# Attention ramp: spare multiplications on TensorE, two projections moved a quad sooner, maxima loaded behind a stack

## The chip, the cores and the metric

The kernel runs on one core of a Trainium2 chip. The metric is the device time of one execution in microseconds (us). The kernel before has a median of 692.57 us over three runs (691.49 to 697.25).

## The reference

One transformer layer on `x` of shape 8 x 512 x 128, in float32: attention with 16 heads of size 8, a residual and a layer norm, then a mixture of experts (one shared and eight routed, two of them per row) with a residual and a layer norm. Only attention is touched by the change:

```python
qkv = x @ w_qkv + b_qkv
qkv = qkv.reshape(B, 16, S, 24)          # 32 rows of x make one head
q, k, v = jnp.split(qkv, 3, axis=-1)     # head dimension 8
attn = jax.nn.softmax(jnp.einsum('bhqd,bhkd->bhqk', q, k) / sqrt(8), axis=-1)
vals = jnp.einsum('bhqk,bhkd->bhqd', attn, v)
x = layernorm(x + vals.transpose(0, 2, 1, 3).reshape(B, S, 128) @ w_out + b_out)
...                                      # mixture of experts, second layer norm
```

## The kernel before

The 4096 rows of `x` are 32 **quads** of 128 rows; one quad holds four heads of 512 positions, and four quads make one batch. Attention is a software pipeline over **stages**: `run_stages` runs stage -4, -3, ... on all engines, and each engine has its instructions of every stage written out in a fixed order. Stage s = 4b + i does, each where the quad exists:

- the projections of quad s + 4: TensorE turns `x` (job `xT`, L506), ScalarE copies it, TensorE multiplies by `wq` and `wk` (job `qkv`, L512, L513) and, for quad s + 1, by `wv` (L517); ScalarE reads the results (L562, L566);
- the split of quad s + 4 into three bf16 parts on GpSimd (L831 to L837), which waits until the parts of the quad before are stored;
- on SyncE's queue: the load of the next 128 rows of `x` (L706), the store of the parts of quad s + 3 (L745), two small loads of the maxima of quad s + 1 into the row stack (L751), then the reads that build the **stack** of quad s + 3, its `qs` (L763, three) and `ks` (L767, five), from the stored parts, and later the expert weights (L725);
- the A scores of quad s + 2 on TensorE (L987, bf16, 72 rows of the array, 512 columns), of which VectorE takes row maxima (L931), eight steps of two matmuls and one reduction; `scoreA` has two banks, so that the A scores of a step wait for the reduction two steps before;
- the maxima of quad s + 1: TensorE turns them (job `mT`, L524, after step 1), VectorE splits and negates them (L599, L601, behind the reduction of step 1), SyncE loads them (L751);
- the B scores of quad s (L1001, 74 rows: 72 and the two of the maxima), which ScalarE exponentiates (L904), and the product with `v` of quad s - 1, called PV here (L1021, float32, 128 rows, four groups of four matmuls, after steps 1, 3, 5 and 7).

So stages -4 to -1 fill the pipe. Stage -2 is the first with A scores (quad 0), stage 0 the first with B scores, stage 1 the first with PV. All jobs of TensorE share one bank, `shared`: a job begins when the one before was read (`job_read`). Their order is the table in `Jobs.at`, which says at which step of which stage each kind stands.

TensorE begins the A scores of a stage once the stack of that quad has landed (L975), and the B scores once the maxima are loaded (L993). SyncE has one queue in order: what stands behind a wait there waits too.

Of the kernel before, what the change touches and what calls it, by code (L numbers as in the profile page):

```python
# [50 lines left out]
class Jobs:  # L51
# [4 lines left out]

    def __init__(self, batches):
        self.quads = 4 * batches  # L60
        self.batches = batches
        self.index = {}
        n = 0
        for s in range(-4, self.quads + 4):
            for at in range(8):
                for kind in self.at(s // 4, s % 4, at):
                    self.index[kind, s] = n
                    n += 1
        self.total = n
        self.period = self.index["mT", 12] - self.index["mT", 8]  # L70

    def at(self, b, i, at):

        inner = not isinstance(b, int)
        s = 4 * b + i if not inner else 8
        kinds = []
        if at == 0 and i == 2 and (inner or 1 <= b <= self.batches):
            kinds.append("proj")
        if at == 5 and i == 3 and (inner or 1 <= b <= self.batches):
            kinds.append("x1T")  # L80
        if at == 1 and (inner or 0 <= s + 1 < self.quads):
            kinds.append("mT")
        if at == 2 and i == 1 and (inner or 2 <= b <= self.batches):
            kinds.append("counts")
        if at == 3 and (inner or 0 <= s - 2 < self.quads):
            kinds.append("valsT")
        if at == 4 and (inner or s + 4 < self.quads):
            kinds.append("xT")
        if at == 7 and i == 3 and (inner or 1 <= b <= self.batches):
            kinds.append("gate")  # L90
        if at == 6 and (inner or s + 4 < self.quads or 0 <= s + 1 < self.quads):
            kinds.append("qkv")
        if at == 7 and i == 1 and (inner or 1 <= b <= self.batches):
            kinds.append("oT")
        return kinds

    def number(self, kind, b, i):

# [6 lines left out]
def layer(nc, x, w_qkv, b_qkv, w_out, b_out, wg, ws1, ws3, ws2, we1, we3, we2, out):  # L105
# [26 lines left out]
    with ctx:  # L132
# [167 lines left out]
        def has(b, i, ahead):  # L300

            return not isinstance(b, int) or 0 <= 4 * b + i + ahead < QUADS

        def finishing(b):

            return not isinstance(b, int) or 1 <= b <= B
# [391 lines left out]
        def attention_sync(sp):  # L698
            sp.dma_start(w_raw[:], w_qkv.rearrange("i (c k d) -> i c k d", k=3, d=HD)).then_inc(qkv_loaded, 16)

            def load_x(b, i):

                if has(b, i, 2):
                    bb, ii = (b, i - 2) if i > 1 else (b - 1, i + 2)
                    need(sp, job_ready, jobs.number("xT", bb, ii) + 1)
                sp.dma_start(xin[:, i % 2, :], x_rows[bass.ds((4 * b + i + 4) * P, P), :]).then_inc(x_loaded[i % 2], 16)  # L706

            load_x(-1, 0)
            load_x(-1, 1)
            bias = b_qkv.rearrange("(c k d) -> c k d", k=3, d=HD)  # L710
            for k in range(2):
                sp.dma_start(bq[:, k:k + 1], bias[:, k, :].rearrange("c d -> d c"), allow_slow_non_contiguous=True) \
                  .then_inc(bias_loaded, 16)
            bias_low = b_qkv.rearrange("(q l k d) -> l k q d", q=NCH, l=4, k=3)
            for low in range(4):
                sp.dma_start(bv[32 * low:32 * low + 32], repeated(bias_low[low, 2], 32)).then_inc(w_loaded, 16)
            sp.dma_start(w_o[:], w_out).then_inc(w_loaded, 16)
            sp.dma_start(b_o[:], b_out.partition_broadcast(P)).then_inc(w_loaded, 16)
            sp.dma_start(w_g[:], wg).then_inc(w_loaded, 16)

            def load_expert_weights(n):

                if n < 2:
                    w, at = (we1, we3)[n], w13[:, 0:E, n, :]
                    sp.dma_start(at, w.rearrange("e d f -> d e f")).then_inc(experts_loaded, 16)  # L725
                elif n < 2 + NFC:
                    c = n - 2
                    sp.dma_start(w2[:, 0:E, c, :], we2[:, c * P:(c + 1) * P, :].rearrange("e f d -> f e d")) \
                      .then_inc(experts_loaded, 16)
                elif n == 2 + NFC:  # L730
                    sp.dma_start(w13[:, E, 0, :], ws1).then_inc(experts_loaded, 16)
                    sp.dma_start(w13[:, E, 1, :], ws3).then_inc(experts_loaded, 16)
                    sp.dma_start(w2[:, E], ws2.rearrange("(c f) d -> f c d", f=P)).then_inc(experts_loaded, 16)

            def stage(b, i):
                q = 4 * b + i
                if has(b, i, 4) and not (isinstance(b, int) and q < -2):
                    load_x(b, i)
                if has(b, i, 3):

                    n, par = q + 3, (i + 3) % 2
                    need(sp, split_done, n + 1)

                    need(sp, stack_loaded[par], 16 * STACK_DMAS * (2 * b + (i + 3) // 2))
                    sp.dma_start(parts_dram[par].rearrange("k h i p t -> p (k h i) t"),  # L745
                                 parts[:].rearrange("p k h i t -> p (k h i) t")).then_inc(parts_stored, 16)
                if has(b, i, 1):

                    sp.wait_ge(job_read, jobs.number("mT", b, i) + 1)
                    for m in range(2):  # L750
                        sp.dma_start(qs[KR + m:KR + m + 1, (i + 1) % 4].rearrange("p h x -> p (h x)"), m2[:, m, :]) \  # L751
                          .then_inc(m_loaded, 16)
                if has(b, i, 3):
                    need(sp, parts_stored, 16 * (n + 1))

                    if has(b, i, -1):
                        need(sp, b_ready, 16 * q)
                    st = (i + 3) % 4
                    if isinstance(b, int) and n < 4:

                        sp.wait_ge(ones_set, n + 1)
                    for r in range(3):
                        sp.dma_start(qs[PR * r:PR * (r + 1), st],  # L763
                                     parts_dram[par, 0].rearrange("h i (d c) t -> (i d) h (c t)", d=HD)) \
                          .then_inc(stack_loaded[par], 16)
                    for row, i0, i1 in K_ROWS:
                        sp.dma_start(ks[row:row + HD * (i1 - i0), st],  # L767
                                     parts_dram[par, 1, :, i0:i1].rearrange("h i (d c) t -> (i d) h (c t)", d=HD)) \
                          .then_inc(stack_loaded[par], 16)
                if finishing(b) and i == 0:  # L770

                    if not isinstance(b, int) or b > 1:
                        need(sp, job_read, jobs.number("proj", b - 1, 2) + 1)
                    for low in range(4):
                        sp.dma_start(xres[32 * low:32 * low + 32], x_perm[b - 1, low]).then_inc(xr_loaded, 16)
                if routing(b) and i == 0:
                    store_x1(sp, b - 1)
                if isinstance(b, int) and 0 <= q < 8:
                    load_expert_weights(q)

            run_stages(sp, stage)

            need(sp, pv_done, QUADS - 1)
            need(sp, x1_stored, 64 * (B - 1))
            for n in range(B - 1):
                load_x1(sp, n)
# [97 lines left out]
        def attention_scalar(act):  # L884
# [3 lines left out]
            def stage(b, i):  # L888
# [8 lines left out]
                for j in range(4):  # L897
                    for u in range(2):
                        for c in range(2):
                            if has(b, i, 0):  # L900
                                act.wait_ge(b_ready, 16 * q + 4 * j + 2 * u + c + 1)
                                if j == 0 and u == 0 and c == 0:
                                    need(act, pv_done, q - 1)
                                act.activation(prob[:, i % 2, j, 2 * u + c, :], scoreB[:, c], ACT.Exp,  # L904
                                               scale=SCALE).then_inc(exp_done, 1)
                        for kind in jobs.at(b, i, 2 * j + u):
                            if kind not in ("valsT", "proj", "mT", "counts"):
                                act_job(act, kind, b, i)

            run_stages(act, stage)  # L910
            x_high(act, 0)
# [5 lines left out]
        def attention_vector(dve):  # L917
# [8 lines left out]
            def stage(b, i):  # L926
                q = 4 * b + i
                for at in range(8):
                    if has(b, i, 2):
                        dve.wait_ge(a_ready, 8 * (q + 2) + at + 1)  # L930
                        dve.tensor_reduce(mx[:, i % 2, at // 2, at % 2 * 2:at % 2 * 2 + 2], scoreA[:, at % 2], AX.X,  # L931
                                          ALU.max).then_inc(max_done, 1)
                    for kind in jobs.at(b, i, at):
                        if kind in ("valsT", "proj", "mT"):
                            dve_job(dve, kind, b, i)

                    if isinstance(b, int) and q == QUADS and at == 7:
                        x_low(dve, 0)
# [32 lines left out]
        def attention_tensor(pe):  # L971

            pe.wait_ge(setup, 2)

            def stage(b, i):  # L975
                q = 4 * b + i
                if has(b, i, 2):

                    pe.wait_ge(stack_loaded[i % 2], 16 * STACK_DMAS * (2 * b + i // 2 + 2))
# [24 lines left out]
                for at in range(8):  # L1004
# [2 lines left out]
                    score_b(at, 0)  # L1007
                    score_a(at, 1)
                    score_b(at, 1)
                    for kind in jobs.at(b, i, at):  # L1010
                        pe_job(pe, kind, b, i)

                    if isinstance(b, int) and q == QUADS and at == 4:
                        turn_x(pe, 0)
# [615 lines left out]
```

## Time and profile before

| | |
|---|---|
| median of three runs | 692.57 us (691.49, 692.57, 697.25) |
| the profiled execution | 700.51 us, span 698.8 us |
| busy share of the span | TensorE 92%, VectorE 79%, ScalarE 61%, GpSimd 39% |
| stages -4 to -1 | 0 to 40.00 us |
| stage 0, stage 1 | 40.00 to 55.61, 55.61 to 73.73 us |
| stages 2 and 3 | from 73.73 and 87.37 us, 13.64 us apart |

The profiled execution is 7.94 us longer than the median and 3.26 us longer than the slowest run shown. Times in the rows are from the start of its span. A busy TensorE is not TensorE at its peak: the page counts a matmul as busy at either clock. The clock that matmuls really ran at is read from the distance between their starts.

### The profile page before, as it was taken

To read this page: it belongs to the slowest core of one execution; us is meant where nothing else is said; L and a number is where in the kernel's file an instruction comes from. 1 tells how busy PE (TensorE), PEld (TensorE's weight loads), DVE (VectorE), ACT (ScalarE), POOL (GpSimd) and SP (SyncE) were. 2 spreads that over 40 slices of the span, in tenths; PEclk is the share of its full clock that TensorE was granted. 3 is DMA by queue.
4 is the path that set the end of the run, shared out by engine and by line. 5 is a ranking of instruction groups with operands and counts; after the bars stand their busy time and mean duration, and the time that the engine had idled before them with its cause. 6 is when DMAs were issued, how large, how long until landed. Compare 5 with 4: busy or idle time off the path is not lost.

```text
span 698.8 us, 16083 instructions
## 1 busy us (share of the span) xinstructions
PE 641.5 (92%) x4593; PEld 313.8 (45%) x4593; DVE 549.5 (79%) x1272; ACT 425.8 (61%) x973; POOL 270.1 (39%) x402
## 2 busy tenths in 40 slices
PE   1899999999899999999999999999899989999970
PEld 1232333343334343343433334323248878888760
DVE  4875777778787998999799799797658757878882
ACT  2055777777567667777676766776734246666652
POOL 3122232122325324423433532440515416677772
PEclk9999999999999999999999999999989999999995
DMA  4366556443414433333332443230132033454522
GB/s 78 58 127 177 127 118 152 106 95 89 83 44 80 101 75 68 90 62 87 80 79 53 84 101 70 65 88 12 52 106 58 27 81 88 121 160 134 155 83 75
DMA packets 161857, 62.68 MB, mean 90 GB/s; under 512 B 110586, under 2 KB 155516, under 8 KB 161808
## 3 DMA queue, kind: packets, MB, share of 16 engines
q1 hardware_dynamic: 155008, 46.72, 30.7%
q0 software_dynamic: 5648, 13.26, 6.2%
q10 hardware_dynamic: 1152, 2.10, 0.8%
q8 instruction: 24, 0.39, 0.3%
q14 instruction: 25, 0.20, 0.1%
HBM read 38.04 MB, written 24.26 MB: 89 GB/s over the span
## 4 chain that ended last, share of the span: by engine, by line
PE 61%; issue 10%; POOL 10%; DMA 6%; DVE 6%; ACT 4%; SPq 2%; POOLq 0%; ACTq 0%; DVEq 0%
PE pvp L1021 17%; PE scoreB L1001 16%; PE scoreA L987 15%; POOL y_dram L1212 6%; DMA parts_dram<-parts 3%; DVE mx L931 2%; ACT prob L904 2%; PE shared L528 2%; POOL slots_dram L491 2%; DMA ks<-parts_dram 2%; PE shared L517 2%; PE shared L536 1%; POOL prob L1197 1%; PE shared L512 1%; PE shared L547 1%
## 5 line engine op out<-in xcount | busy, mean ns | idle before, releaser
L931 DVE TENSOR_REDUCE mx<-scoreA 128x2 f32<-128x1024 f32 x256 | 305.6, 1219 | 73.7 <-PE scoreA L987 71.2
L904 ACT ACTIVATE prob<-scoreB 128x512 f32<-128x512 f32 x512 | 279.7, 600 | 122.4 <-PE scoreB L1001 122.0
L987 PE MATMUL scoreA<-ks,qs 72*128 72x512 bf16 x512 | 206.6, 411 | 15.9 <-DMA ks<-parts_dram 13.4
L1001 PE MATMUL scoreB<-qs,ks 74*128 74x512 bf16 x512 | 201.6, 396 | 6.3 <-ACT prob L904 3.0
L1021 PE MATMUL pvp<-prob,v 128*32 128x512 f32 x1024 | 139.9, 620 | 0.8 <-ACT pv_sb L896 0.8
L987 PEld LDWEIGHTS scoreA<-ks,qs 72*128 72x128 bf16 x512 | 51.2, 102 | 158.1 <-DVE mx L931 73.8
L1001 PEld LDWEIGHTS scoreB<-qs,ks 74*128 74x128 bf16 x512 | 50.0, 99 | 102.1 <-ACT prob L904 79.0
L1212 POOL DMA_INDIRECT y_dram<-prob x72 | 70.9, 985 | 44.9 <-issue 30.3
L831 POOL CAST parts<-qk 128x256 bf16<-128x256 f32 x32 | 12.7, 398 | 187.9 <-ACT v_raw L566 168.4
L491 POOL DMA_INDIRECT slots_dram<-rows,slot_i x64 | 63.4, 991 | 55.9 <-DMA ks<-parts_dram 30.8
L1571 PE MATMUL scoreB<-w,prob 128*128 x288 | 44.0, 276 | 0.9 <-DVE prob L1384 0.9
L1440 ACT ACTIVATE prob<-scoreA 128x256 f32<-128x256 f32 x72 | 27.6, 384 | 22.8 <-PE pvp L1559 10.7
L1571 PEld LDWEIGHTS scoreB<-w,prob 128*128 128x128 f32 x288 | 37.8, 191 | 1.2 <-issue 1.1
L1549 PE MATMUL scoreA<-w_high,ebT_high 128*128 x72 | 34.6, 480 | 3.9 <-DVE gated L1388 3.8
L1388 DVE TENSOR_TENSOR gated<-scoreA,prob 128x256 f32<-128x256 f32 x72 | 30.1, 418 | 8.2 <-ACT prob L1440 7.8
L1021 PEld LDWEIGHTS pvp<-prob,v 128*32 128x32 f32 x1024 | 20.4, 109 | 30.3 <-issue 28.8
L1447 ACT ACTIVATE prob<-scoreB,prob 128x128 f32<-128x128 f32 x72 | 26.7, 370 | 11.4 <-PE scoreA L1529 9.1
L639 POOL TENSOR_SCALAR veps<-mv 128x4 f32<-128x4 f32 x8 | 1.8, 228 | 76.7 <-DVE mv L621 76.7
L562 ACT ACTIVATE qk<-shared,bq 128x128 f32<-128x128 f32 x64 | 20.0, 364 | 17.9 <-PE shared L517 12.2
L1318 DVE TENSOR_TENSOR ebT_low<-scoreA,ebT_high 128x128 fp32r<-128x128 f32 x72 | 20.7, 289 | 10.3 <-ACT ebT_high L1414 8.7
L1551 PE MATMUL scoreA<-w_high,ebT_low 128*128 x72 | 28.4, 394 | 0.0
L1550 PE MATMUL scoreA<-w_low,ebT_high 128*128 x72 | 28.3, 393 | 0.0
(174 smaller groups left out, 892.8 us busy)
## 6 DMA issues: line engine op xcount, KB each, us to landing
qs<-parts_dram SPq DMA_DIRECT2D x96, 96.0 KB
parts_dram<-parts SPq DMA_DIRECT2D x32, 192.0 KB
slots_dram<-blank POOLq DMA_DIRECT2D x9, 520.0 KB
prob<-slots_dram SPq DMA_DIRECT2D x72, 65.0 KB, 1.9
ks<-parts_dram SPq DMA_DIRECT2D x64, 64.0 KB
prob<-y_dram SPq DMA_DIRECT2D x8, 512.0 KB
ks<-parts_dram SPq DMA_DIRECT2D x32, 96.0 KB
xin<-in_L_attn_x SPq DMA_DIRECT2D x32, 64.0 KB, 2.2
```

The costliest lines, as they stand in the source:

```text
L491: pool.indirect_dma_start(slots_dram, bass.IndirectOffsetOnAxis(ap=slot_i[:, j, t:t + 1], axis=0), rows[:, t, j, :], None).then_inc(scatte ...
L904: act.activation(prob[:, i % 2, j, 2 * u + c, :], scoreB[:, c], ACT.Exp, scale=SCALE).then_inc(exp_done, 1)
L931: dve.tensor_reduce(mx[:, i % 2, at // 2, at % 2 * 2:at % 2 * 2 + 2], scoreA[:, at % 2], AX.X, ALU.max).then_inc(max_done, 1)
L987: ins = pe.matmul(scoreA[:, at % 2, c], qs[0:KR, st, j, qc * P:(qc + 1) * P], ks[0:KR, st, j, :], start=True, stop=True)
L1001: pe.matmul(scoreB[:, c], ks[0:KM, i, j, kc * P:(kc + 1) * P], qs[0:KM, i, j, :], start=True, stop=True).then_inc(b_ready, 1)
L1021: ins = pe.matmul(pvp[32 * h:32 * h + 32, :], v[:, (i - 1) % 2, h, j, :], prob[:, (i - 1) % 2, h, j, :], start=(j == 0), stop=(j == 3))
L1212: pool.indirect_dma_start(y2_dram, bass.IndirectOffsetOnAxis(ap=eb[:, at, D:D + 1].bitcast(I32), axis=0), yo[:, r, :], None, bounds_check= ...
L1388: dve.tensor_tensor(gated[:, r % 4, :], h_bank(r)[:, F:2 * F], silu[:, r % 2, :], ALU.mult) \
L1549: pe.matmul(h, ebT_highs[:, r % 4], high, start=True, stop=False)
L1550: pe.matmul(h, ebT_highs[:, r % 4], low, start=False, stop=False)
L1551: ins = pe.matmul(h, ebT_lows[:, r % 4], high, start=False, stop=True)
L1571: ins = pe.matmul(y_bank(r), gatedT[:, (r - 4) % 4, c * P:(c + 1) * P], w2_flat[:, bass.ds(e * NFC * D + c * D, D)], start=(c == 0), stop= ...
```

## The change

Quads are counted from 0, so "quads 3 and 4" of the summary are quads 2 and 3 here.

- `Jobs.SOONER` moves the jobs `xT` and `qkv` of quad 2 from stage -2 (steps 4 and 6) to step 7 of stage -3, and those of quad 3 from stage -1 to steps 4 and 6 of stage -2. The multiplication by `wv` for quad 0 goes along with quad 3. Their `x` is loaded at the start of stage -3.
- In stage -1 (the only one with `ramp` and maxima) SyncE loads the maxima of quad 0 behind the stack of quad 2 and not ahead of it.
- TensorE gets spare multiplications, whose results in `pvp` nobody reads: four of the identity by itself (128 columns), one of `wq` by the raw weights (384 columns) in stage -3 ahead of `xT` of quad 2, eight (384 columns) at the start of stage -2, thirteen of 256 columns at the steps of stages -2 and -1 that have no job, and four of 256 columns in stage 0, after each odd step. All are float32 with 128 rows.

TensorE around the start of stage -2, where `xin` is `x` as loaded, `shared` the bank of the jobs and `pvp` the bank that PV uses from stage 1 on; before:

```order
L506 MATMUL shared<-ident,xin 128x128
L512 MATMUL shared<-xT,wq 128x128
L513 MATMUL shared<-xT,wk 128x128
L987 MATMUL scoreA<-ks,qs 128x512 x10
L506 MATMUL shared<-ident,xin 128x128
L987 MATMUL scoreA<-ks,qs 128x512 x4
L512 MATMUL shared<-xT,wq 128x128
L513 MATMUL shared<-xT,wk 128x128
L987 MATMUL scoreA<-ks,qs 128x512 x6
```

and changed (line numbers of the changed file):

```order
L512 MATMUL shared<-ident,xin 128x128
L518 MATMUL shared<-xT,wq 128x128
L519 MATMUL shared<-xT,wk 128x128
L995 MATMUL pvp<-w_raw,wq 128x384
L512 MATMUL shared<-ident,xin 128x128
L518 MATMUL shared<-xT,wq 128x128
L519 MATMUL shared<-xT,wk 128x128
L995 MATMUL pvp<-w_raw,wq 128x384 x8
L1012 MATMUL scoreA<-ks,qs 128x512 x2
L995 MATMUL pvp<-w_raw,wq 128x256
```

The first three rows are quad 1 in both. Quad 2's turn and projections now stand ahead of the first A scores, and nine spare multiplications around them.

SyncE's queue in stage -1, where `m2` holds the split maxima; before:

```order
L706 DMA xin<-in_L0_attn_x 128x128
L745 DMA parts_dram<-parts 128x24x32
L751 DMA qs<-m2 1x16x128 x2
L763 DMA qs<-parts_dram 24x4x512 x3
L767 DMA ks<-parts_dram 24x4x512
L767 DMA ks<-parts_dram 16x4x512
L767 DMA ks<-parts_dram 8x4x512 x2
L767 DMA ks<-parts_dram 16x4x512
```

and changed:

```order
L754 DMA parts_dram<-parts 128x24x32
L776 DMA qs<-parts_dram 24x4x512 x3
L780 DMA ks<-parts_dram 24x4x512
L780 DMA ks<-parts_dram 16x4x512
L780 DMA ks<-parts_dram 8x4x512 x2
L780 DMA ks<-parts_dram 16x4x512
L760 DMA qs<-m2 1x16x128 x2
```

The load of `x` has gone (it stands ahead of the first store of parts now), and the two loads of maxima have moved from ahead of the eight reads of the stack to behind them.

The diff, without the loops that only unpack the longer tuples of `jobs.at`:

```diff
+    SOONER = [("xT", 2, -3, 7), ("qkv", 2, -3, 7), ("xT", 3, -2, 4), ("qkv", 3, -2, 6)]
...
+        early = not inner and s in (-2, -1)
...
-        if at == 4 and (inner or s + 4 < self.quads):
+        if at == 4 and not early and (inner or s + 4 < self.quads):
             kinds.append("xT")
...
-        if at == 6 and (inner or s + 4 < self.quads or 0 <= s + 1 < self.quads):
+        if at == 6 and not early and (inner or s + 4 < self.quads or 0 <= s + 1 < self.quads):
             kinds.append("qkv")
...
-        return kinds
+        own = [(kind, b, i) for kind in kinds]
+        if not inner:
+            own += [(kind, -1, ii) for kind, ii, stage, step in self.SOONER if (stage, step) == (s, at)]
+        return own
...
         def attention_sync(sp):
...
             def stage(b, i):
                 q = 4 * b + i
-                if has(b, i, 4) and not (isinstance(b, int) and q < -2):
+                if isinstance(b, int) and q == -3:
+                    load_x(-1, 2)
+                    load_x(-1, 3)
+                if has(b, i, 4) and not (isinstance(b, int) and q < 0):
                     load_x(b, i)
...
-                if has(b, i, 1):
+                def load_maxima():
...
+                ramp = isinstance(b, int) and q < 0
+                if has(b, i, 1) and not ramp:
+                    load_maxima()
                 if has(b, i, 3):
...
+                if has(b, i, 1) and ramp:
+                    load_maxima()
...
         def attention_tensor(pe):
             pe.wait_ge(setup, 2)
+            for n in range(4):
+                pe.matmul(pvp[:, 0:P], ident[:], ident[:], start=True, stop=True)
+            def warm(times, columns):
+                for n in range(times):
+                    pe.matmul(pvp[:, 0:columns], wq[:], w_raw[:].rearrange("p c k d -> p (c k d)")[:, 0:columns],
+                              start=True, stop=True)
             def stage(b, i):
                 q = 4 * b + i
+                if isinstance(b, int) and q == -2:
+                    warm(8, 3 * P)
...
+                    for kind, bb, ii in jobs.at(b, i, at):
+                        if kind == "xT" and isinstance(b, int) and q == -3 and at == 7:
+                            warm(1, 3 * P)
+                        pe_job(pe, kind, bb, ii)
+                    if isinstance(b, int) and q in (-2, -1) and not jobs.at(b, i, at) or \
+                            isinstance(b, int) and q == 0 and u:
+                        warm(1, 2 * P)
```

## Rows read from the trace of the kernel before

**Rows 1.** The page's first part: busy us, share, instructions.

```profile
PE 641.5 (92%) x4593; PEld 313.8 (45%) x4593; DVE 549.5 (79%) x1272; ACT 425.8 (61%) x973; POOL 270.1 (39%) x402
```

**Rows 2.** Windows: stretch, length, busy PE PEld DVE ACT POOL, clock, DMA, GB/s.

```profile
40.00:50.00 10.00, 10.00 (x25) 3.62 (x26) 7.11 (x8) 6.14 (x11) 2.85 (x5) 1.00 0.56 112
```

**Rows 3.** Timeline of TensorE, 40 to 88 us: start, length, line, tiles.

```profile
40.00 0.61 PE L987 MATMUL scoreA<-ks,qs 72*128 72x512 bf16 x1 [0.74 <-DMA ks<-parts_dram]
...
55.61 0.63 PE L987 MATMUL scoreA<-ks,qs 72*128 72x512 bf16 x1
...
59.38 1.94 PE L1021 MATMUL pvp<-prob,v 128*32 128x512 f32 x8
...
64.77 1.94 PE L1021 MATMUL pvp<-prob,v 128*32 128x512 f32 x8
66.64 0.59 PE L987 MATMUL scoreA<-ks,qs 72*128 72x512 bf16 x1
...
73.73 0.39 PE L987 MATMUL scoreA<-ks,qs 72*128 72x512 bf16 x1
...
87.37 0.39 PE L987 MATMUL scoreA<-ks,qs 72*128 72x512 bf16 x1
```

**Rows 4.** The chain that ended last, 26 to 80 us: start, length, what.

```profile
26.46 0.43 PE shared L512 x2
...
70.99 0.22 PE shared L512 x2
...
79.11 0.44 PE shared L528 x4
```

**Rows 5.** Timeline of TensorE around 190 us.

```profile
189.79 0.47 PE L987 MATMUL scoreA<-ks,qs 72*128 72x512 bf16 x1 [2.17 <-DMA ks<-parts_dram]
...
191.34 1.91 PE L536 MATMUL shared<-w_o,valsT 128*128 128x128 f32 x8
...
193.43 0.38 PE L1001 MATMUL scoreB<-qs,ks 74*128 74x512 bf16 x1
```

**Rows 6.** Timeline of TensorE, the first 20 us.

```profile
6.24 0.48 PE L506 MATMUL shared<-ident,xin 128*128 128x128 f32 x1 [0.72 <-ACT qk L562]
...
7.66 0.64 PE L513 MATMUL shared<-xT,wk 128*128 128x128 f32 x2
18.29 1.89 PE L987 MATMUL scoreA<-ks,qs 72*128 72x512 bf16 x4 [9.99 <-DMA ks<-parts_dram]
```

**Rows 7.** Timeline of VectorE, 19 to 41 us.

```profile
19.43 8.29 DVE L931 TENSOR_REDUCE mx<-scoreA 128x2 f32<-128x1024 f32 x7 [8.34 <-PE scoreA L987]
...
31.70 0.27 DVE L599 TENSOR_SCALAR m<-shared 16x128 bf16<-16x128 f32 x1
...
39.30 1.23 DVE L931 TENSOR_REDUCE mx<-scoreA 128x2 f32<-128x1024 f32 x1 [1.18 <-PE scoreA L987]
```

**Rows 8.** Timeline of SyncE's queue, 23 to 50 us: when it issues, how long.

```profile
23.24 0.43 SPq L706 DMA_DIRECT2D xin<-in_L_attn_x  x1
30.42 0.38 SPq L745 DMA_DIRECT2D parts_dram<-parts  x1
...
34.17 1.15 SPq L763 DMA_DIRECT2D qs<-parts_dram  x3
35.37 1.83 SPq L767 DMA_DIRECT2D ks<-parts_dram  x5
...
44.96 1.44 SPq L751 DMA_DIRECT2D qs<-m  x2
46.49 1.39 SPq L763 DMA_DIRECT2D qs<-parts_dram  x3
47.92 1.83 SPq L767 DMA_DIRECT2D ks<-parts_dram  x5
```

**Rows 9.** Stage 5: the chain's longest transfer, and TensorE at the next stage's start.

```profile
116.07 7.80 DMA parts_dram<-parts
...
129.46 0.39 PE L987 MATMUL scoreA<-ks,qs 72*128 72x512 bf16 x1 [0.50 <-DMA ks<-parts_dram]
```

More of the change, by code:

```diff
@@ L65, in __init__ @@
             for at in range(8):
-                for kind in self.at(s // 4, s % 4, at):
-                    self.index[kind, s] = n
+                for kind, b, i in self.at(s // 4, s % 4, at):
+                    self.index[kind, 4 * b + i] = n
                     n += 1
@@ L905, in stage @@
                                                scale=SCALE).then_inc(exp_done, 1)
-                        for kind in jobs.at(b, i, 2 * j + u):
+                        for kind, bb, ii in jobs.at(b, i, 2 * j + u):
                             if kind not in ("valsT", "proj", "mT", "counts"):
-                                act_job(act, kind, b, i)
+                                act_job(act, kind, bb, ii)
             run_stages(act, stage)
@@ L932, in stage @@
                                           ALU.max).then_inc(max_done, 1)
-                    for kind in jobs.at(b, i, at):
+                    for kind, bb, ii in jobs.at(b, i, at):
                         if kind in ("valsT", "proj", "mT"):
-                            dve_job(dve, kind, b, i)
+                            dve_job(dve, kind, bb, ii)
                     if isinstance(b, int) and q == QUADS and at == 7:
@@ L1009, in stage @@
                     score_b(at, 1)
-                    for kind in jobs.at(b, i, at):
-                        pe_job(pe, kind, b, i)
+                    for kind, bb, ii in jobs.at(b, i, at):
+                        if kind == "xT" and isinstance(b, int) and q == -3 and at == 7:
[4 more added lines that the diff above has]
+                        warm(1, 2 * P)
                     if isinstance(b, int) and q == QUADS and at == 4:
```

## The prediction

> **What bounds the kernel now.** I read the page's table of engines first, then the windows of the first 100 us, the timelines of TensorE, VectorE and SyncE's queue there, and last the chain of waits. The table says that TensorE is busy 92% of the span [rows 1], which hides the point: TensorE's busy time counts at either clock. In the window 40 to 50 us TensorE is busy 10.00 of 10.00 us and the column of the granted clock reads 1.00 [rows 2], yet the matmuls there run at half rate. A 128-column float32 multiplication takes 0.43 us of the chain at 26 us and 0.22 us at 71 us [rows 4]: those are the 1.2 and the 2.4 GHz level, so the clock column is no help in this stretch and the durations decide. The timeline shows the change of level: the first A score that follows the second PV group starts at 66.64, takes 0.59 where 0.63 was usual, and 0.39 is usual afterwards [rows 3]. So everything up to 66.64 us, the whole filling of the pipe and most of two stages, ran at 1.2 GHz. At 2.4 GHz a stage takes 13.64 us (73.73 to 87.37); stage 0 took 15.61 (40.00 to 55.61) and stage 1 18.12 (55.61 to 73.73) [rows 3].
>
> What did TensorE do before the clock rose? From 40.00 it was busy without a pause with A and B scores, which use 72 and 74 of 128 rows, and stayed low; the rise falls into a float32 group of 128 rows [rows 3]. At 189.79 it is low again, after a pause of 2.17 us, and is high at 193.43, after 1.91 us of float32 projections with 128 rows [rows 5]. Both rises follow float32 work on all rows. The spare multiplications are of that kind (128 rows, 128 columns of weights, as L536 has).
>
> **The change part by part.** Sizes: a spare of 384 columns is three times 0.43 or 0.22, so 1.29 us low and 0.66 high; one of 256 columns 0.86 or 0.44 [rows 4].
>
> *The first spares.* Four of 0.43 us fit between the identity and the arrival of `x`, at nothing; if they were late, every stage would be late by that, 0.3 us at most. The one of 1.29 us runs from 8.30, the end of quad 1's projections [rows 6], to 9.59, and hides the load of quad 2's `x`. From the turn of quad 1 to the end of its projections 2.06 us pass (6.24 to 8.30) [rows 6], so quad 2's end at about 11.7. Then come the eight: 10.3 us all low, 5.3 all high, so they end between 17.0 and 22.0, where the first stack lands at 18.29 [rows 6]. Which? At 190 us the clock came back 3.6 us after TensorE resumed [rows 5]. With 3.6 us of low work here, the other 6.7 us halve to 3.35, and the eight end at 18.6: **0.3 us late**, bounds 0 and 3.7.
>
> *Stages -2 and -1.* VectorE sets the pace here: seven reductions in 8.29 us, 1.184 each [rows 7]. Per step TensorE has two A scores and one spare: 0.44 + 0.44 = 0.88 at 2.4 GHz, hidden; 1.72 at 1.2 GHz, not hidden. I take them at nothing; the other end is a rival. The first reduction comes some 0.6 us after the first A score (1.14 before), at 19.2. Sixteen reductions and the split of the maxima (two of 0.27 us [rows 7]) take 19.5 us, so all are done at 38.7; before it was 39.30 + 1.23 = 40.53 [rows 7]. The 1.8 us come from the gaps that low-clock projections left.
>
> *The stack of quad 2.* Before, its parts were stored at 30.42 and its reads issued from 34.17 to 37.20, and stage 0 waited for it until 40.00, 2.8 us after the last issue [rows 3, 8]. Now the parts are ready when SyncE is through with stack 1, at about 23.2 [rows 8]. With the same distances (3.75 from store to first read, 3.03 of issue, 2.8 to land) the stack lands at about 33, and the maxima of quad 0, split at about 31.5, land behind it at 35 to 37. Both are ahead of the 37.5 at which the bank for stage 0's first A score comes free, so this wait goes. What is late next is VectorE. GpSimd's clearing of slots (520 KB) also moves here and shares the engines; I cost it at nothing, the cover being 1 to 4 us.
>
> *Stage 0* then goes at VectorE's pace: its first two reductions end at 41.1, the maxima of quad 1 are split at 41.6. The next bound is SyncE's queue, where for this stage the maxima still stand ahead of stack 3: from the maxima's issue to the end of the stack's it is 44.96 to 49.75, 4.8 us [rows 8], and 2.8 to land. Stage 1 begins at 49.2 (41.6 + 4.8 + 2.8) instead of 55.61: **6.4 us**. The four spares (1.8 us) lie beside that wait.
>
> *Stage 1* at 2.4 GHz takes a normal 13.64 us less the turn of PV results, which it doesn't have (0.44 us [rows 4]): 13.2, ending at 62.4 instead of 73.73. The gain so far is **11.3 us**.
>
> *Given back:* SyncE loads 1 MB of expert weights behind the stack in stages 0 and 1. Shorter stages bring them closer to the next store of parts. Stage 5 shows the price: a store that took 7.80 us, and the next stage began at 129.46 where three normal stages after 87.37 give 128.29 [rows 3, 9], 1.17 us late. That can happen in none, one or both of these stages, 0 to 2.3 us; I take one. Net 10.1 us.
>
> **Against which time.** The sum is made in an execution of 700.51 us, so such an execution would take 690.4. It lies 7.94 us above the median; part of that is the pause at 187 to 193 us, which the change doesn't touch. But the late rise may be part of it too: had the clock risen in the first PV group, at 61.3 [rows 3], the 5.3 us to 66.64 would have taken half, and there would be 2.7 us less to win. Not knowing which holds in the runs of the median, I take half: a gain of 8.8 us, **683.8 us**. Later stages gain and lose nothing: each waits on the one before, none on a fixed time.
>
> **A rule against this.** From 3.49 us on, at every matmul up to 66.64 us, the rows show the low level: 9.5% of the span, of which the 26.6 us from 40.00 on were all busy at half rate [rows 2, 3]. The Trainium skill, "TensorE: Matmul & The Clock Gate", section "What's actually happening", says that for modelling the penalty of the ramp is under 1% of a typical kernel's span. By that rule less than 6.9 us could be won and the time would be 685.7 or more; by the rows it is the 8.8 above. The rows of one execution disagree with it, but they are of one execution: a rival below.
>
> **The rivals.**
> - *The clock falls again* (0.14). In stages -2 and -1 TensorE works only 0.88 of each 1.18 us. Each fall costs 0.54 us a step while it lasts, and the one at 190 us lasted about three steps [rows 5], so 1.6; two or three falls take 4 us: 687.7. For it: the pause of 2.17 us at 187.6 was enough. Against: no pause here is over 0.4 us.
> - *Transfers take over* (0.12): expert weights in both stages, clearing of slots against stack 2 and the maxima: 2 to 4 us more, 686 to 688.
> - *The ramp's penalty is small in ordinary runs* (0.07): the clock rises before stage 1 there, by busy time alone, so that stages 0 and 1 lose less at half rate than in this execution. If it rose halfway through stage 0, the 8 us to its end and 11 us of stage 1 would have taken half; what is left is the 1.8 us of VectorE and some of stack 3's wait: 3 to 5 us, 688 to 690.
> - *Slower* (0.05): the spares don't raise the clock. It decides at about 22 us: if A scores still take 0.86 a pair there, the eight end at 22.0 (3.7 late), stage -2 takes 13.7 us (eight pairs 6.9, six spares 5.2, projections 1.7), stage -1 13.1, stage 0 15.6 + 3.4; stage 1 begins at 67.8 instead of 55.61, 12.2 us later: 704.8. For it: 26 busy us that did not raise it. Against: both rises shown followed work like the spares.
>
> **How the numbers follow.** The forecast has 0.62, and its own range is 680.3 (the 11.3 us and one more) to 686. The rivals at 686 to 690 hold 0.33 together; 679.5 to 689.5 leaves out the slower case and some at each edge. A measurement of this kernel can't tell less than about 1% from no change, so faster means under 685.6 and slower over 699.5. Faster: the forecast nearly whole and some of the transfers, 0.64; slower 0.05; same 0.31.
>
> **What would show it.** In the trace of the changed kernel: A scores of stage -2 at 0.39 us and not 0.63; the eight spares ending near 18.6; reductions back to back from 19.2 to 38.7; no wait of TensorE on stack 2; stage 1 beginning near 49 behind stack 3, and stage 2 near 62 to 63.5. Wrong would be: A scores at 0.63 after 22 us (the spares don't act); spares that VectorE waits for; a stage 0 that waits for the maxima of quad 0; or the right starts of stages with the same total, which would say that the median runs had less to lose.

## The result

The changed kernel takes 685.99 us (median of four runs, 683.56 to 689.05) where the kernel before takes 694.09 in the same comparison: a ratio of 0.9881, interval 0.9847 to 0.9916, so about 1.2% or 8.1 us faster. In a second comparison, on the chip of the second group of experiments, it was 688.67 against 695.79: 0.9909, interval 0.9875 to 0.9944. Forecast were 683.8 us and 8.8 us of gain. The profiled execution of the changed kernel has a span of 684.5 us and a time of 686.20. The ratios leave out executions more than 1.5% above the fastest of their kernel: four of ten of the kernel with only the spares, and one of ten (737.85 us) of the kernel with only the first spares.

**Filling the pipe.** TensorE's timeline of the changed kernel, first 36 us (it answers to [rows 6]; A scores are L1012 here, spares L990 and L995):

```profile
1.58 2.08 PE L990 MATMUL pvp<-ident 128*128 128x128 f32 x8 [1.58 <-POOL ident L806]
3.48 0.48 PE L512 MATMUL shared<-ident,xin 128*128 128x128 f32 x1
...
11.39 7.08 PE L995 MATMUL pvp<-w_raw,wq 128*128 128x384 f32 x16
18.31 0.60 PE L1012 MATMUL scoreA<-ks,qs 72*128 72x512 bf16 x2
18.75 0.60 PE L995 MATMUL pvp<-w_raw,wq 128*128 128x256 f32 x2
```

The eight spares (two records each) would take 10.3 us low and take about 7.0: the clock rises among them, and the first A score follows at 18.31. A pair of A scores takes 0.60 us from its first start to its last end, where two pairs took 1.89 before [rows 6]. VectorE has no gap any more (its reductions are L946, the split of the maxima L605; compare [rows 7]):

```profile
19.02 11.41 DVE L946 TENSOR_REDUCE mx<-scoreA 128x2 f32<-128x1024 f32 x10 [7.93 <-PE scoreA L1012]
30.34 0.27 DVE L605 TENSOR_SCALAR m<-shared 16x128 bf16<-16x128 f32 x1
...
30.85 9.12 DVE L946 TENSOR_REDUCE mx<-scoreA 128x2 f32<-128x1024 f32 x8
39.90 0.27 DVE L605 TENSOR_SCALAR m<-shared 16x128 bf16<-16x128 f32 x1
```

**SyncE's queue** (L754 stores parts, L776 and L780 read the stack, L760 loads maxima, L731 expert weights; it answers to [rows 8]):

```profile
22.92 0.38 SPq L754 DMA_DIRECT2D parts_dram<-parts  x1
27.02 1.13 SPq L776 DMA_DIRECT2D qs<-parts_dram  x3
28.19 1.83 SPq L780 DMA_DIRECT2D ks<-parts_dram  x5
30.95 1.96 SPq L760 DMA_DIRECT2D qs<-m  x2
...
40.51 1.15 SPq L760 DMA_DIRECT2D qs<-m  x2
41.75 1.32 SPq L776 DMA_DIRECT2D qs<-parts_dram  x3
43.12 1.84 SPq L780 DMA_DIRECT2D ks<-parts_dram  x5
45.00 0.43 SPq L731 DMA_DIRECT2D w<-in_L_ffn_We  x1
...
49.32 0.37 SPq L754 DMA_DIRECT2D parts_dram<-parts  x1
51.08 2.97 SPq L760 DMA_DIRECT2D qs<-m  x2
56.59 1.15 SPq L776 DMA_DIRECT2D qs<-parts_dram  x3
```

Stack 2 is read from 27.02 instead of 34.17, and nobody waits for it. But the store of quad 4's parts, issued at 49.32, lets the reads of stack 4 go only at 56.59, 7.27 us later, where 3.75 was the distance in [rows 8]. TensorE waits for it (timeline of TensorE, 47 to 81 us, PV is L1051; compare [rows 3]):

```profile
47.33 0.39 PE L1012 MATMUL scoreA<-ks,qs 72*128 72x512 bf16 x1
...
59.53 1.06 PE L1051 MATMUL pvp<-prob,v 128*32 128x512 f32 x8
62.18 0.39 PE L1012 MATMUL scoreA<-ks,qs 72*128 72x512 bf16 x1 [1.58 <-DMA ks<-parts_dram]
...
62.96 0.63 PE L1026 MATMUL scoreB<-qs,ks 74*128 74x512 bf16 x1
...
73.29 0.39 PE L1012 MATMUL scoreA<-ks,qs 72*128 72x512 bf16 x1
...
80.17 0.39 PE L1012 MATMUL scoreA<-ks,qs 72*128 72x512 bf16 x1
```

Stage 1 begins at 47.33, stage 2 at 62.18 after a pause of 1.58 us. After the pause the matmuls are 0.63 long again, and stage 2 lasts 17.99 us (62.18 to 80.17) instead of 13.64. The windows show the fall in the clock column (columns as in [rows 2]):

```profile
58.00:62.00 4.00, 2.60 (x47) 0.86 (x45) 2.06 (x2) 2.84 (x7) 2.21 (x5) 1.00 0.61 152
62.00:66.00 4.00, 3.82 (x13) 1.23 (x17) 2.31 (x2) 2.39 (x4) 1.17 (x2) 0.59 1.08 290
66.00:70.00 4.00, 4.00 (x15) 0.96 (x8) 1.79 (x4) 1.19 (x2) 0.00 (x0) 0.50 1.00 151
70.00:74.00 4.00, 4.00 (x19) 1.44 (x17) 1.81 (x4) 1.26 (x3) 0.00 (x0) 0.63 0.38 112
```

The table has the time at which VectorE splits the maxima in a stage, once a stage, so that two kernels can be laid side by side (the last column is the best kernel of the experiments):

| stage | before | changed | gain | clearing moved |
|---|---|---|---|---|
| -1 | 31.70 | 30.34 | 1.36 | 30.18 |
| 0 | 44.35 | 39.90 | 4.45 | 39.74 |
| 1 | 59.98 | 50.46 | 9.52 | 50.25 |
| 2 | 76.86 | 66.06 | 10.80 | 63.46 |
| 3 | 90.50 | 83.31 | 7.19 | 77.10 |
| 9 | 176.25 | 168.62 | 7.63 | 162.49 |
| 10 | 195.21 | 184.52 | 10.69 | 178.05 |
| 30 | 484.36 | 473.93 | 10.43 | 467.45 |

The change gains 10.8 us up to stage 2 and gives 3.6 back in stage 2. The 14.3 us between the two profiled executions are more than that: 3.1 come at stage 10, where the execution before had a pause and a fall of its own [rows 5], and the rest behind stage 30. I don't count those as the change's; 7.2 to 7.6 us are, beside medians that differ by 8.1 and 7.1.

### The profile page after: what moved, and what is told of

Same layout as the page of the kernel before. It is cut to its first block, busy times and chain, and to the rows that moved or that the text cites. A ratio compares the mean times of both kernels' runs of the same rounds, so it can differ in the third digit from the quotient of the medians.

```text
span 684.5 us, 16202 instructions
## 1 busy us (share of the span) xinstructions
PE 640.4 (94%) x4653; PEld 320.8 (47%) x4653; DVE 548.9 (80%) x1272; ACT 424.2 (62%) x973; POOL 269.4 (39%) x402
## 4 chain that ended last, share of the span: by engine, by line
PE 64%; issue 11%; POOL 8%; DVE 7%; DMA 4%; ACT 4%; SPq 2%; POOLq 0%; ACTq 0%; DVEq 0%
PE pvp L1051 16%; PE scoreB L1026 15%; PE scoreA L1012 14%; POOL y_dram L1242 6%; DVE mx L946 4%; DMA parts_dram<-parts 3%; ACT prob L919 2%; PE shared L534 2%; PE scoreB L1527 2%; PE shared L523 2%; PE pvp L995 1%; PE shared L518 1%; PE shared L553 1%; POOL prob L1227 1%; PE shared L542 1%
## 5 line engine op out<-in xcount | busy, mean ns | idle before, releaser
L946 DVE TENSOR_REDUCE mx<-scoreA 128x2 f32<-128x1024 f32 x256 | 304.5, 1219 | 65.1 <-PE scoreA L1012 62.5
L1026 PE MATMUL scoreB<-qs,ks 74*128 74x512 bf16 x512 | 197.0, 387 | 6.4 <-ACT prob L919 3.0
L1012 PE MATMUL scoreA<-ks,qs 72*128 72x512 bf16 x512 | 195.2, 386 | 4.7 <-DMA ks<-parts_dram 2.4
L1051 PE MATMUL pvp<-prob,v 128*32 128x512 f32 x1024 | 137.6, 611 | 0.8 <-ACT pv_sb L911 0.8
L1012 PEld LDWEIGHTS scoreA<-ks,qs 72*128 72x128 bf16 x512 | 49.6, 99 | 138.9 <-DVE mx L946 65.1
L1051 PEld LDWEIGHTS pvp<-prob,v 128*32 128x32 f32 x1024 | 20.4, 108 | 29.4 <-issue 27.8
```

Source lines behind the costliest of these rows:

```text
L1012: ins = pe.matmul(scoreA[:, at % 2, c], qs[0:KR, st, j, qc * P:(qc + 1) * P], ks[0:KR, st, j, :], start=True, stop=True)
L1026: pe.matmul(scoreB[:, c], ks[0:KM, i, j, kc * P:(kc + 1) * P], qs[0:KM, i, j, :], start=True, stop=True).then_inc(b_ready, 1)
L1051: ins = pe.matmul(pvp[32 * h:32 * h + 32, :], v[:, (i - 1) % 2, h, j, :], prob[:, (i - 1) % 2, h, j, :], start=(j == 0), stop=(j == 3))
```

## The experiments

Ratios are to the kernel before, with intervals, each within its group on one chip.

**Only the spares.** The order of jobs and SyncE's queue as before, twelve spares of 384 columns instead of nine:

```diff
-    SOONER = [("xT", 2, -3, 7), ("qkv", 2, -3, 7), ("xT", 3, -2, 4), ("qkv", 3, -2, 6)]
+    SOONER = []
-        early = not inner and s in (-2, -1)
+        early = False
-                if isinstance(b, int) and q == -3:
-                    load_x(-1, 2)
-                    load_x(-1, 3)
-                if has(b, i, 4) and not (isinstance(b, int) and q < 0):
+                if has(b, i, 4) and not (isinstance(b, int) and q < -2):
-                ramp = isinstance(b, int) and q < 0
+                ramp = False
-                    warm(8, 3 * P)
+                    warm(12, 3 * P)
```

> The changed kernel with the order of jobs and of SyncE's queue put back as before; the spares stay, twelve instead of nine of 384 columns ahead of the first A scores, since TensorE idles longer there. Theory (most of the gain is the clock, the moved work gives about 3 us): stage 0 still starts near 40, held by the stack of quad 2, but at 2.4 GHz, its maxima are loaded about 3 us later than in the changed kernel, stage 1 starts near 50.2 and stage 2 near 64: some 5 us faster than before, 3 us slower than the changed kernel (ratio to before 0.992). Rival (the moved work is what pays, and the clock would have come by itself): ratio 0.997 or more.

Measured: 695.44 us, 0.9978 (0.9934 to 1.0022); single times from 686.53, at a mean granted clock of 0.986, to 701.21 at 0.954. The medians, over all ten, differ by 0.1% only (694.79 before). The number is the rival's, but neither theory had the mechanism: the clock rises early, but stage 0 still pauses for stack 2 (1.72 us in the profiled execution, which is the longest of the ten), the clock falls there, and stages 0 and 1 run low after all. The one run with a clock of 0.986 has the gain; the other nine, at 0.975 and less, don't.

**Only the moved work.** No spare at all:

```diff
-            for n in range(4):
-                pe.matmul(pvp[:, 0:P], ident[:], ident[:], start=True, stop=True)
-                if isinstance(b, int) and q == -2:
-                    warm(8, 3 * P)
-                        if kind == "xT" and isinstance(b, int) and q == -3 and at == 7:
-                            warm(1, 3 * P)
-                    if isinstance(b, int) and q in (-2, -1) and not jobs.at(b, i, at) or \
-                            isinstance(b, int) and q == 0 and u:
-                        warm(1, 2 * P)
```

> The changed kernel without any spare. Theory: the A and B scores run at 1.2 GHz until PV, as before; stage 0 starts near 37.5 instead of 40.0 since the stack of quad 2 is no longer late, but takes 15.6 us, and stage 1 18: 2 to 2.5 us faster than before (ratio 0.997). Rival (the moved work pays most): ratio 0.990 or less, as the changed kernel.

Measured: 695.80 us, 1.0009 (0.9974 to 1.0043). The rival falls; the theory's 2 us can't be seen. TensorE's timeline of this kernel (PV is L1041, B scores L1021):

```profile
58.09 1.94 PE L1041 MATMUL pvp<-prob,v 128*32 128x512 f32 x8
59.95 0.61 PE L1007 MATMUL scoreA<-ks,qs 72*128 72x512 bf16 x1
...
61.21 0.48 PE L1021 MATMUL scoreB<-qs,ks 74*128 74x512 bf16 x1
61.52 0.38 PE L1007 MATMUL scoreA<-ks,qs 72*128 72x512 bf16 x1
```

Here the clock rises behind the first PV group of stage 1, where in [rows 3] it was the second. So the late rise of the execution before is one of at least two cases.

**Spares on 64 rows**, same number and columns:

```diff
-                    pe.matmul(pvp[:, 0:columns], wq[:], w_raw[:].rearrange("p c k d -> p (c k d)")[:, 0:columns],
+                    pe.matmul(pvp[:, 0:columns], wq[0:64, :], w_raw[0:64].rearrange("p c k d -> p (c k d)")[:, 0:columns],
```

> The changed kernel with the spares on 64 of the 128 rows (half of the weights and of the moving data), same number, columns and so time. Theory (it is work on all rows that was done ahead of each rise seen): the clock does not rise in the eight spares, they end near 22, A scores still take 0.63 in stage -2, stage 1 starts near 68; 10 us slower than before (ratio 1.014). Rival (TensorE being busy is enough): the same as the changed kernel (0.988).

Measured: 712.36 us, 1.026 (1.0193 to 1.0327). TensorE's timeline:

```profile
11.80 10.61 PE L995 MATMUL pvp<-w_raw,wq 64*128 64x384 f32 x16
22.33 1.03 PE L1012 MATMUL scoreA<-ks,qs 72*128 72x512 bf16 x2
23.30 1.22 PE L995 MATMUL pvp<-w_raw,wq 64*128 64x256 f32 x2
```

The eight take 10.61 us, a pair of A scores still 1.03: no rise. Being busy is not enough, as theory had it, and this is the prediction's slower case on the chip: spares that don't raise the clock cost 17 to 18 us, more than the 12.2 reckoned. Part of that is the edit itself: a spare of 256 columns on 64 rows takes 1.15 us of TensorE's time, from its start to that of the next A score (23.30 to 24.45), where 0.86 was reckoned and one on 128 rows at half rate took 0.85 in the kernel with only the spares (42.01 to 42.86). Stage 1 begins at 75.05 here, not at the 67.8 of the prediction.

**Only the first spares.** The spares at the steps of stages -2, -1 and 0 go; the four, the one and the eight stay (the first clause of the expectation, on thirteen places, is badly put):

```diff
-                    if isinstance(b, int) and q in (-2, -1) and not jobs.at(b, i, at) or \
-                            isinstance(b, int) and q == 0 and u:
-                        warm(1, 2 * P)
```

> The changed kernel with the thirteen spares ahead of their first thirteen places only: the four, the one and the eight stay, those at the steps of stages -2, -1 and 0 go. Theory (A scores at VectorE's pace, 0.44 of each 1.18 us on 72 rows, don't hold the clock up): it rises in the eight, falls again in stage -2 or -1, stages 0 and 1 run at 1.2 GHz; as slow as the changed kernel without any spare, 0.999. Rival (once up, only a pause of TensorE brings it down): the clock stays up, 0.986 to 0.988.

Measured: 694.67 us, 0.9969 (0.9937 to 1.0001). Windows of this kernel:

```profile
14.00:18.00 4.00, 4.00 (x14) 2.17 (x13) 0.00 (x0) 0.62 (x2) 0.75 (x2) 1.00 0.87 147
18.00:22.00 4.00, 2.51 (x9) 0.54 (x8) 3.29 (x3) 0.00 (x0) 1.88 (x4) 0.87 0.38 84
22.00:26.00 4.00, 3.80 (x11) 1.53 (x11) 4.00 (x5) 0.28 (x1) 0.25 (x1) 0.50 0.81 126
...
66.00:70.00 4.00, 4.00 (x15) 1.04 (x13) 2.45 (x2) 2.38 (x5) 0.00 (x0) 0.50 0.74 249
```

The clock rises in the eight and falls at 21 us with the first A scores at VectorE's pace, whose pauses are under 1 us, and stays low to about 72 us. The thirteen spares in the steps of stages -2 and -1 hold it up; that the four of stage 0, which went with them, have no part in it is the next run.

**The four spares of stage 0 out:**

```diff
-                    if isinstance(b, int) and q in (-2, -1) and not jobs.at(b, i, at) or \
-                            isinstance(b, int) and q == 0 and u:
+                    if isinstance(b, int) and q in (-2, -1) and not jobs.at(b, i, at):
```

> The changed kernel without the four spares of stage 0. Theory (with A and B scores together TensorE has hardly a gap, so the clock that is up stays up, and the stage goes at VectorE's pace and waits for stack 3 in any case): the same as the changed kernel, 0.988 to 0.991. Rival (scores on 72 rows don't hold it): the clock falls in stage 0, 4 to 8 us lost, 0.996 or more.

Measured: 686.80 us, 0.9879 (0.9842 to 0.9915), as the changed kernel. They neither cost nor give anything that can be measured. In its profiled execution the clock stays up all through stage 0, with A and B scores and the usual jobs alone. Later it passes one pause and falls after a shorter one (timeline of TensorE):

```profile
77.10 0.39 PE L1012 MATMUL scoreA<-ks,qs 72*128 72x512 bf16 x1 [1.79 <-DMA ks<-parts_dram]
...
163.56 0.39 PE L1012 MATMUL scoreA<-ks,qs 72*128 72x512 bf16 x1 [1.29 <-DMA ks<-parts_dram]
```

After 77.10 the matmuls stay at the high level; from 164.85 they are 0.63 long.

**Maxima ahead of the stack again**, all else as changed:

```diff
-                ramp = isinstance(b, int) and q < 0
+                ramp = False
```

> The changed kernel with the loads of the maxima put back ahead of the stack of quad 2 in stage -1. Theory: the reads of stack 2 issue from 32.9 instead of 27.0 and land near 38.7, where TensorE could go on at 36.7; a pause of 2 us ahead of stage 0, the clock falls there as it did with the spares alone, stages 0 and 1 run at 1.2 GHz: 0.996 to 0.999. Rival (the pause alone, the clock stays up): 2 us more than the changed kernel, 0.992 to 0.994.

Measured: 697.59 us, 1.0041 (1.0014 to 1.0067). TensorE's timeline and windows:

```profile
35.52 0.60 PE L995 MATMUL pvp<-w_raw,wq 128*128 128x256 f32 x2
39.21 0.61 PE L1012 MATMUL scoreA<-ks,qs 72*128 72x512 bf16 x1 [3.10 <-DMA ks<-parts_dram]
```

```profile
34.00:38.00 4.00, 2.02 (x8) 0.93 (x8) 3.28 (x3) 0.00 (x0) 0.00 (x0) 0.96 0.74 166
38.00:42.00 4.00, 2.79 (x7) 0.96 (x8) 1.23 (x1) 1.20 (x3) 0.00 (x0) 0.50 0.50 47
...
62.00:66.00 4.00, 4.00 (x16) 0.84 (x15) 1.89 (x4) 1.55 (x3) 0.32 (x2) 0.63 0.60 149
```

The order of SyncE's queue in one stage decides the whole gain: a pause of 3.10 us ahead of stage 0, the clock falls, and it is low until 65 us.

**What holds up the store of quad 4's parts.** First suspect: the 1 MB of expert weights behind stack 3.

```diff
-                if n < 2:
-                    w, at = (we1, we3)[n], w13[:, 0:E, n, :]
-                    sp.dma_start(at, w.rearrange("e d f -> d e f")).then_inc(experts_loaded, 16)
+                if n < 4:
+                    k, e0 = n // 2, n % 2 * (E // 2)
+                    sp.dma_start(w13[:, e0:e0 + E // 2, k, :],
+                                 (we1, we3)[k][e0:e0 + E // 2].rearrange("e d f -> d e f")).then_inc(experts_loaded, 16)
...
-                if isinstance(b, int) and 0 <= q < 8:
-                    load_expert_weights(q)
+                if isinstance(b, int) and 1 <= q < 8:
+                    load_expert_weights(q - 1)
```

> The changed kernel, with the two expert weight loads of 1 MB cut into halves of 512 KB, and the whole series of loads begun in stage 1 instead of stage 0 (none behind the stack of stage 0). Theory (the 1 MB load behind stack 3 delays the store of quad 4's parts, so stack 4 is late, TensorE pauses 1.6 us and the clock falls for 10 us): the store takes under 5.5 us instead of 7.25, stage 2 starts near 60.6 without a pause, the clock stays up, stage 3 starts near 74.3 instead of 80.2; 5 to 6 us faster than the changed kernel (ratio to before 0.980). Rival (the clearing of slots by GpSimd holds the store up): store and pause as in the changed kernel, same time (0.988).

Measured: 683.64 us, 0.984 (0.9776 to 0.9903). The theory of the store fell: it is as long as in the changed kernel, and the pause is still 1.23 us. Yet the clock stayed up in the profiled execution, and the four single runs have a mean clock of 0.985 to 0.988, where the changed kernel's have 0.978 to 0.987; the interval holds theory's time and the rival's. Second suspect: GpSimd's clearing of slots, 520 KB, issued at 49.65 us in the changed kernel, 0.3 us behind the store. It was first moved to the start of every stage, alone and with the halves:

```diff
+                if isinstance(b, int) and -1 <= q < SLOTS // 8 - 1:
+                    pool.wait_ge(stack_loaded[i % 2], 16 * STACK_DMAS * (2 * b + i // 2 + 2))
+                    clear_slots(q + 1)
...
-                if isinstance(b, int) and -1 <= q < SLOTS // 8 - 1:
-                    clear_slots(q + 1)
```

> The changed kernel, with GpSimd's clearing of slots (520 KB a stage) moved from the end of its work of a stage, where it meets the store of parts, to the start of the stage, behind the arrival of the stack that TensorE waits for. Theory after the halves (the clearing that starts 0.3 us behind the store of quad 4's parts makes it 7.25 us long): the store takes 4 to 5.5 us (the 1 MB of weights is still ahead of it), stage 2 begins near 60.6 without a pause or with one under 0.5 us, the clock stays up there; 683 us, 0.983. Rival (weights and clearing each suffice to delay the store): the pause stays at 1 us or more, time as the changed kernel.

> The clearing at the start of the stage, and the weights in halves from stage 1 on. Both theories: the store of quad 4's parts meets neither and takes 4 us, stage 2 begins near 60.6 with no pause, clock up; 682 to 683 us, 0.982. If the store is still 7 us long, neither transfer is the cause.

Measured: 685.63 us, 0.9862 (0.9822 to 0.9903), and 681.91 us, 0.9819 (0.9784 to 0.9854). Both edits missed their aim: GpSimd reaches the start of stage 1 late, and clears at 51.77 and 51.22, still beside the store (7.04 and 7.24 us, pauses 1.31 and 1.41). By the last expectation neither transfer would be the cause; but the store did meet the clearing. So, for stage 0 alone, the clearing was moved to the start, where it went out at 32.72 with the halves and at 36.13 without:

```diff
+                if isinstance(b, int) and q == 0:
+                    pool.wait_ge(stack_loaded[0], 16 * STACK_DMAS * 2)
+                    clear_slots(1)
...
-                if isinstance(b, int) and -1 <= q < SLOTS // 8 - 1:
+                if isinstance(b, int) and -1 <= q < SLOTS // 8 - 1 and q != 0:
                     clear_slots(q + 1)
```

> The changed kernel with neither transfer beside the store of quad 4's parts (about 49 us): the weights in halves from stage 1 on, and GpSimd's clearing of stage 0 moved from its end to its start, behind the arrival of stack 2 (about 35 us); the other clearings stay where the changed kernel has them. Theory (those two hold the store up, and so make the pause and the fall of the clock): the store takes 4 to 4.5 us instead of 7.2, stage 2 begins near 60.6 without a pause behind stack 4, the clock stays up; 681 to 682 us, 0.980 to 0.982. Rival (the store is slow for a reason of its own, as the two kernels before let one think): 7 us again and a pause of 1.2 us or more, 0.984.

> The clearing of stage 0 moved as in the kernel before this one, the 1 MB of weights left behind stack 3 where the changed kernel has it. With the halves (only the clearing was left, 7.26 us) this makes the four cases. Theory (the clearing is what holds the store up; the weights are through by 50 us): 4 to 5 us for the store, pause under 0.5 us, 0.982. Rival (either is enough): 6 us or more, pause as in the changed kernel, 0.988.

Measured: 683.61 us, 0.9833 (0.9805 to 0.9861), without weights and clearing beside the store; 680.96 us, 0.9815 (0.9789 to 0.9841), with the weights alone. SyncE's queue, from the store's issue to the first read of stack 4, in the kernel with the clearing alone (the halves):

```profile
49.20 0.38 SPq L755 DMA_DIRECT2D parts_dram<-parts  x1
51.34 2.60 SPq L761 DMA_DIRECT2D qs<-m  x2
56.46 1.15 SPq L777 DMA_DIRECT2D qs<-parts_dram  x3
```

with the weights alone:

```profile
49.17 0.37 SPq L754 DMA_DIRECT2D parts_dram<-parts  x1
50.86 2.25 SPq L760 DMA_DIRECT2D qs<-m  x2
54.61 1.15 SPq L776 DMA_DIRECT2D qs<-parts_dram  x3
```

and with neither:

```profile
49.04 0.38 SPq L755 DMA_DIRECT2D parts_dram<-parts  x1
50.92 1.22 SPq L761 DMA_DIRECT2D qs<-m  x2
52.79 1.14 SPq L777 DMA_DIRECT2D qs<-parts_dram  x3
```

The four cases: 7.27 us with both, 7.26 with the clearing, 5.44 with the weights, 3.75 with neither; pauses ahead of stage 2 of 1.58, 1.23, none and none. In these stages the pause comes with the clearing. But meeting it is not all. In the kernel before, the clearing (L813, GpSimd) met the same store just as closely (timeline of GpSimd and SyncE's queue):

```profile
57.31 0.37 SPq L745 DMA_DIRECT2D parts_dram<-parts  x1
57.64 0.88 POOL L813 DMA_DIRECT2D slots_dram<-blank  x1
...
62.18 1.33 SPq L763 DMA_DIRECT2D qs<-parts_dram  x3
```

There the reads went out 4.87 us after the store and SyncE had no wait for it. What makes it 7.26 in the changed stages is open.

Stage 3's maxima come at 83.31, 78.86, 77.10 and 77.15. With the clearing moved and nothing else, stages 2 and 3 follow without a pause and the clock holds from 14.3 us to the end of TensorE's work in the profiled execution: 1.85% faster than before. It has the lowest median here, 680.96 us; the kernel with clearing at the start and halves, at 0.9819, can't be told from it, though its store was 7.24 us long and its pause 1.41: its clock stayed up there too.

**The changed kernel again**, beside the two kernels with the clearing at the start and the one with the first spares:

> The changed kernel as it is, on the same chip as the three that follow. All theories: 0.988 of the time before, stage 2 begins after a pause of 1.6 us behind stack 4; whether the clock then falls differs from execution to execution, so the single times spread over 683 to 689.

Measured: 688.67 us (687.63 to 689.80), 0.9909. The pause was 2.09 us, and the clock fell again. The single times spread over 2.2 us and not over the 6 expected, all at a mean clock of 0.978 to 0.980.

## Why the prediction was right

The time lies in the range and the mechanism is as forecast up to stage 2, but that the total is so near (8.1 us of gain for 8.8) is in part luck: two terms were off in opposite directions. So is stage 2's start at 62.18, inside the forecast 62 to 63.5: the work was done 1.8 us sooner, and a pause took most of that back.

- *First spares*: forecast to end at 18.6, 0.3 late; the first A score starts at 18.31 (18.29 before). Right.
- *VectorE sets the pace, back to back, 19.2 to 38.7*: it starts at 19.02 and has no gap, but a reduction comes every 1.14 us (11.41 for ten, 9.12 for eight) and not every 1.184, most likely because the seven of [rows 7] had short waits for A scores in them, which no row shows one by one. The maxima of quad 1 are split from 39.90 instead of 41.1, 1.2 us better than forecast.
- *Stage 0 waits for stack 3 behind the maxima*: stage 1 begins at 47.33 instead of 49.2. The queue took 4.45 us instead of 4.8 (40.51 to 44.96) and the landing 2.4 instead of 2.8.
- *Stage 1 in 13.2 us*: 47.33 to the end of its work at 60.60 (62.18 less the pause) is 13.27. Right. Up to here the gain is 13.1 us, where 11.3 was forecast.
- *Given back, 1.17 us for one late store*: this is the step that failed in size. The price was read from a stage that ran late by the pause alone [rows 9]. Here the pause was 1.58 us, and the clock fell with it: 4.35 us more in stage 2, 5.9 in all. I had blamed the expert weights; with the clearing of slots moved the pause goes, with the weights moved it stays. The clearing I had costed at nothing and looked for only beside stack 2. Pause and fall were each in a rival, but not that the first can bring the second, though [rows 5] shows just that.
- *Half of the 2.7 us of a late rise*: the kernel without spares rose behind the first PV group, so both cases exist. Which of them the runs of the median have was not measured.
- *What raises the clock*: spares on 128 rows did, and on 64 did not, as forecast. But [rows 3] also has a PV group on 128 rows, at 59.38, that no rise followed; the prediction passed over it. And the 9.5% of the rule against it counts from 0; from 3.49 to 66.64 us it is 9.0%.
- *Which part pays*: I added the clock and the queue as terms of a sum. They are not: spares alone give 0.9978, moved work alone 1.0009, all but the queue's order 1.0041, all together 0.988 to 0.991. A pause ahead of stage 0 undoes the spares. The spares and the queue's order without the two projections moved were not run, so what the projections give stays open.

The rival of the small penalty is out: up to 1.85% (0.9815) is to be had in the ramp by clock and queue together, and neither profiled execution without spares rose before 61 us. The Trainium skill, "TensorE: Matmul & The Clock Gate", section "What's actually happening", puts the penalty of the ramp under 1% of a typical span; the measurement disagrees for this kernel. The same section has the warming up go by time, whatever is issued; 10.61 us of spares on 64 rows did not raise the clock, and the same on 128 rows did.

## What to carry to other kernels

Read the clock of a filling pipe from the distance between matmuls, not from their busy time. Where spare work is to raise it, give it all rows, keep some of it where TensorE works in pieces at another engine's pace (the thirteen were needed, the four of stage 0 were not), and then remove the pauses behind it: not each was followed by a fall, but one of 1.6 us cost 4.4 us more at half rate. When stages get shorter, look for transfers of other queues beside the ones on the path: with one clearing of 520 KB moved from the end of its stage to the start, the gain between medians was 13.8 us, where the change alone had 7.1 to 8.1.

## What was not expected of the hardware

- TensorE was busy for 10.61 us with float32 spares on 64 rows without a rise, and in the kernel before from 40.00 to 59.38 us with scores on 72 and 74 rows and some 2 us of jobs on 128 rows between them; it rose within the 7.08 us of spares on 128 rows.
- Work on all rows is not enough by itself either: a first PV group (1.94 us) passed without a rise in the kernel before [rows 3], and three did in the profiled execution of the kernel with only the first spares, which rose at 72 us.
- Once the clock was up, the scores that had not raised it did not let it fall: in the kernel without the spares of stage 0 it stayed up from 36.65 to 49.65 us, where the first PV group starts, through pauses of 0.60 and 0.71.
- The length of a pause does not tell whether a fall follows. Pauses of 1.58, 1.72, 2.09 and 3.10 us were followed by one in the profiled executions, pauses of 0.90, 1.23, 1.31 and 1.41 ahead of stage 2 were not; but the kernel without the spares of stage 0 passed one of 1.79 and fell after one of 1.29. With A scores alone it fell at pauses under 1 us. What decides is left open.
- A store of 192 KB, from its issue to the first read behind it, took 3.75 us alone and 7.26 us beside 520 KB that another queue moved, though it was issued first; in the kernel before it was through within 4.87 us beside the same 520 KB.
